# Two-block parts, resident activations and doubled statistics in a mixed feed-forward after local attention

## The reference

```
x = x + LN(attention(LN(x), w_qkv))                    # 4 x 2048 tokens of width 512, window 128
x = x + LN(ffn(LN(x)))                                 # LN: layer norm over the width, no gain
ffn(y):                                                # for each of 4 batches b
  g   = mean_s(relu(y @ gate_w1.T + gate_b1) @ gate_w2.T + gate_b2)      # 8 numbers for a batch
  mW1 = W1 + sum_e g[e] TW1[e]; mb1 = b1 + g @ Tb1      # 8 experts, mixed into one matrix
  mW2 = W2 + sum_e g[e] TW2[e]; mb2 = b2 + g @ Tb2
  out = gelu(y @ mW1.T + mb1) @ mW2.T + mb2             # hidden width 2048
```

## Time and profile before

| what | value |
|---|---|
| time of the profiled execution | 3095.89 us |
| its span | 3094.1 us |
| mean granted TensorE clock | 0.974 |
| TensorE busy | 2929.2 us (95%) |
| VectorE busy | 1999.8 us (65%) |
| ScalarE busy | 1520.0 us (49%) |
| GpSimd busy | 880.2 us (28%) |
| data moved | 814.49 MB |

### The profile page before, as it was taken

How to read it: one execution, slowest core, us unless ns; L and a number is a source line. 1 busy time by engine, 2 the same in 40 slices (tenths; PEclk the granted TensorE clock), 3 DMA queues, 4 the chain that set the end, 5 groups by cost and what they waited for, 6 DMA issues and landing times.

```text
span 3094.1 us, 55462 instructions
## 1 busy us (share of the span) xinstructions
PE 2929.2 (95%) x20444; PEld 2425.8 (78%) x20444; DVE 1999.8 (65%) x3732; ACT 1520.0 (49%) x2950; POOL 880.2 (28%) x773
## 2 busy tenths in 40 slices
PE   7999999789999999959888899999999999999997
PEld 5888888578888888847776688878888888888886
DVE  4333333278888888857756677798868766897412
ACT  2222222167666666745534455554445544554444
POOL 0000000178888888853310000140005100240004
PEclk9999999889999999979988999999999999999999
DMA  5554554567877777669999999999989988999533
GB/s 190 177 176 163 180 194 167 162 167 197 197 194 186 195 193 188 172 205 363 354 354 348 334 378 381 355 404 403 394 302 352 366 301 316 361 372 356 202 109 123
DMA packets 444433, 814.49 MB, mean 263 GB/s; under 512 B 29705, under 2 KB 161801, under 8 KB 444185
## 3 DMA queue, kind: packets, MB, share of 16 engines
q1 hardware_dynamic: 360800, 630.95, 61.8%
q10 hardware_dynamic: 73920, 146.81, 13.3%
q0 software_dynamic: 9472, 33.56, 2.9%
HBM read 642.89 MB, written 167.78 MB: 262 GB/s over the span
## 4 chain that ended last, share of the span: by engine, by line
PE 42%; DMA 7%; DVE 3%; ACT 1%; issue 1%; POOL 1%; SPq 1%; POOLq 0%; ACTq 0%; DVEq 0%
PE e_hid L1190 7%; PE e_hid L1191 7%; PE e_hid L1192 7%; PE e_acc L1209 7%; PE e_acc L1207 7%; PE e_acc L1208 7%; DMA yl_scratch<-e_yt_lo 4%; DMA e_y_lo<-yl_scratch 3%; DVE e_yt_lo L1441 1%; DVE e_part L1491 1%; DVE e_c_stats L1414 1%; SPq L976 0%; DVE e_c_y L1435 0%; ACT e_yt_hi L1269 0%; POOL e_sums L1111 0%
## 5 line engine op out<-in xcount | busy, mean ns | idle before, releaser
L1491 DVE SCALAR_TENSOR_TENSOR e_part<-e_ring,e_g_cols,e_part 128x512 f32<-128x512 f32 x896 | 659.2, 794 | 6.6 <-DMA e_ring<-mix_rows 4.0
L666 DVE TENSOR_REDUCE b_neg_max<-b_ps_score 128x1 f32<-128x384 f32 (+1 forms) x1024 | 491.7, 527 | 67.6 <-PE b_ps_score L531 56.1
L1305 ACT ACTIVATE e_u<-e_hid,e_mb 128x512 f32<-128x512 f32 x256 | 176.5, 689 | 647.7 <-PE e_hid L1192 644.8
L637 ACT ACTIVATE b_probs<-b_ps_keys 128x384 f32<-128x384 f32 (+1 forms) x1024 | 426.8, 478 | 78.8 <-PE b_ps_keys L546 51.1
L1515 DVE TENSOR_TENSOR e_u_lo<-e_u,e_u_hi 128x512 fp32r<-128x512 f32 x256 | 186.7, 729 | 374.0 <-ACT e_u_hi L1309 373.9
L1099 POOL TENSOR_SCALAR e_var<-e_moments 128x4 f32<-128x4 f32 x16 | 8.1, 504 | 1199.5 <-DVE e_moments L1526 1199.5
L531 PE MATMUL b_ps_score<-b_k_st,b_q_st 96*128 96x384 f32 (+1 forms) x1024 | 333.3, 366 | 15.4 <-DMA b_q_st<-qk_scratch 15.1
L491 POOL TENSOR_TENSOR b_total<-b_probs 128x512 f32<-128x512 f32 x256 | 323.8, 1280 | 64.8 <-ACT b_probs L637 64.8
L546 PE MATMUL b_ps_keys<-b_q_st,b_k_st 97*128 97x384 f32 (+1 forms) x1024 | 315.1, 350 | 23.8 <-DMA b_q_st<-b_max_rows 22.4
L1190 PE MATMUL e_hid<-e_y_hi,e_wb_hi 128*128 128x512 f32 x784 | 308.7, 394 | 22.4 <-DMA e_y_lo<-yl_scratch 13.5
L237 DVE TENSOR_TENSOR a_qk<-a_acc,a_qk 128x512 fp32r<-128x512 f32 x128 | 88.6, 692 | 357.6 <-ACT a_qk L176 356.6
(11 more groups left out here) (137 smaller groups left out, 5837.1 us busy)
## 6 DMA issues: line engine op xcount, KB each, us to landing
e_ring<-mix_rows SPq DMA_DIRECT2D x558, 512.0 KB, 8.9
e_y_hi<-yh_scratch ACTq DMA_DIRECT2D x70, 1024.0 KB, 11.2
e_y_lo<-yl_scratch ACTq DMA_DIRECT2D x70, 1024.0 KB, 17.2
qk_scratch<-a_qk SPq DMA_DIRECT2D x128, 512.0 KB, 2.7
b_k_st<-qk_scratch SPq DMA_DIRECT2D x192, 256.0 KB, 4.2
b_q_st<-qk_scratch SPq DMA_DIRECT2D x192, 256.0 KB, 4.2
a_x_in<-x SPq DMA_DIRECT2D x16, 1024.0 KB, 7.0
v_scratch<-a_v SPq DMA_DIRECT2D x64, 256.0 KB, 3.0
```

The costliest lines, as they stand in the source:

```text
L637: act.activation(probs[:, m % RING, h, 0:(hi - lo) * WIN], ps_keys[x % BANKS][:, 0:(hi - lo) * WIN], ACT.Exp, scale=SCALE).then_inc(exp_do ...
L666: dve.tensor_reduce(neg_max[:, g % 2, i, h:h + 1], ps_score[y % BANKS][:, 0:(hi - lo) * WIN], AX_X, ALU.max, negate=True).then_inc(reduced, 1)
L1491: dve.scalar_tensor_tensor(out=part[:, n % 2, half, :], in0=ring[:, slot, :], scalar=g_cols[:, b, e:e + 1], in1=so_far, op0=ALU.mult, op1= ...
```

## The change

Every unit has two blocks, so that there are 128 runs of two steps in place of 72 of two to four. All four chunks of y of a batch have a place on chip and are loaded once for a batch: chunks 0 and 1 of batch 0 by SP as before, now behind the last transposes of the gate, chunks 2 and 3 by SP behind refill_half(1) and refill_half(2), and those of the next batch by ScalarE after the last hidden_block of the closing run that has the same chunk. W_RING falls from 9 to 5. The statistics have two buffers, used in turn by closing runs, and row_stats waits for the closing run before the last. The wait for the stores of y of all chunks moves from SP to ScalarE's first copy_out.

```diff
-W_RING = 9
+W_RING = 5
...
-    return [(0, 0, 2), (0, 2, 2), (0, 4, 3), (0, 7, 3), (0, 10, 3), (0, 13, 3)] + \
-        [(b, 4 * quarter, 4) for b in range(1, BATCH) for quarter in range(4)]
+    return [(b, j, 2) for b in range(BATCH) for j in range(0, FF // P, 2)]
...
-        stats = sb("stats", [P, TILES, 6], F32)
+        stats = sb("stats", [P, 2, TILES, 6], F32)
...
-        y_hi = sb("y_hi", [P, 2, KD, CH], F32R)
-        y_lo = sb("y_lo", [P, 2, KD, CH], F32R)
+        y_hi = sb("y_hi", [P, PER, KD, CH], F32R)
+        y_lo = sb("y_lo", [P, PER, KD, CH], F32R)
...
-        def load_y(eng, r):
+        def load_y(eng, b, q):
+
+            rows = slice((PER * b + q) * CH, (PER * b + q + 1) * CH)
             for src, dst in ((yh_dram, y_hi), (yl_dram, y_lo)):
-                eng.dma_start(dst[:, r % 2].bitcast(F32),
-                              src[:, tokens(r)].rearrange("(k p) t -> p k t", p=P)).then_inc(y_loaded[r % 2], 16)
+                eng.dma_start(dst[:, q].bitcast(F32),
+                              src[:, rows].rearrange("(k p) t -> p k t", p=P)).then_inc(y_loaded[q], 16)
...
                         sp.wait_ge(x1_done, TILES * CHUNKS)
-                        sp.wait_ge(yt_stored[0], 32)
-                        load_y(sp, 0)
-                        sp.wait_ge(yt_stored[1], 32)
-                        load_y(sp, 1)
+                        sp.wait_ge(turned, KD * CHUNKS)
+                        for q in range(2):
+                            sp.wait_ge(yt_stored[q], 32)
+                            load_y(sp, 0, q)
...
-                for p in range(2):
-                    sp.wait_ge(yt_stored[p], 32 * CHUNKS // 2)
+                sp.wait_ge(yt_stored[0], 64)
+                load_y(sp, 0, 2)
                 refill_half(2)
+                sp.wait_ge(yt_stored[1], 64)
+                load_y(sp, 0, 3)
...
-                    if jj == 0:
-                        pe.wait_ge(y_loaded[r % 2], 32 * (r // 2 + 1))
+                    q = runs[r][1]
+                    if jj == 0 and opens(r):
+                        pe.wait_ge(y_loaded[q], 32 * (batch_of(r) + 1))
...
-                    if s == last[r] and r + 2 < RUNS:
-                        load_y(act, r + 2)
+                    if s == last[r] and closes(r) and b + 1 < BATCH:
+                        load_y(act, b + 1, runs[r][1])
...
                         act.wait_ge(bias_done, biases_by(1))
+                        for p in range(2):
+                            act.wait_ge(yt_stored[p], 32 * CHUNKS // 2)
...
-                    if at:
-                        dve.wait_ge(norm_done, TILES * at)
+                    i = at % 2
+                    if at >= 2:
+                        dve.wait_ge(norm_done, TILES * (at - 1))
```

More of the change, by code:

```diff
@@ L833, in phase_gate_ffn @@
         unused = sb("unused", [P, TILES], F32)
-        stats = sb("stats", [P, TILES, 6], F32)
-        moments = sb("moments", [P, TILES, 2], F32)
-        var = sb("var", [P, TILES], F32)
-        rstd = sb("rstd", [P, TILES], F32)
-        shift = sb("shift", [P, 2, TILES], F32)
+        stats = sb("stats", [P, 2, TILES, 6], F32)
+        moments = sb("moments", [P, 2, TILES, 2], F32)
+        var = sb("var", [P, 2, TILES], F32)
+        rstd = sb("rstd", [P, 2, TILES], F32)
+        shift = sb("shift", [P, 2, 2, TILES], F32)
         c_b1 = sb("c_b1", [P, KD], F32)
@@ L925, in phase_gate_ffn @@
         table_ready = sem("table_ready")
-        y_loaded = [sem(f"y_loaded{i}") for i in range(2)]
+        y_loaded = [sem(f"y_loaded{i}") for i in range(PER)]
         mix_done = sem("mix_done")
@@ L1344, in normalise @@
                         rows = sums[:, runs[r][1], t, :]
-                        act.activation(rows, rows, ACT.Identity, bias=shift[:, 1, t:t + 1], scale=rstd[:, t:t + 1]).then_inc(norm_done, 1)
+                        act.activation(rows, rows, ACT.Identity, bias=shift[:, at % 2, 1, t:t + 1], scale=rstd[:, at % 2, t:t + 1]).then_inc(norm_done, 1)
                 for k in range(-3, CHUNKS):
```

19 lines of the change are left out of this document (10 added, 9 removed).

## The result

The changed kernel takes 3103.23 us (median of 20 runs, 3095.61 to 3113.23), the kernel before 3095.36 in the runs beside it: ratio 1.0024, 95% interval 1.0013 to 1.0034. It is slower by 0.24%, 7.9 us; forecast were 18.7 us. Its profiled execution was its longest, 3113.23 us with a span of 3111.3. How much it loses is known no better than to some 0.2%.

The account below looks back on a forecast made before the run. TensorE was taken to bound the feed-forward, so only its waits and the slow clock behind them could be won. Removed -33.1, closing runs +35.1, tail +16.7 make +18.7 us: 3114 us, range 3084 to 3136.

Parts of the forecast that it names:

- The removed waits: Batch 0: TensorE's waits for y (20.2 us with slow clock) and for block 6 (8.9 us) go.
- moved at no cost: SP's later y loads and stores, and W_RING = 5, would stay covered and cost nothing.
- The closing runs: Ends of batches 0 to 2: late GpSimd costs 11.7 us a batch, 35 in all; the old pattern's 4.0 us go.
- The clock: Behind the stalls at ends of batches 0 to 2: two groups at lower clock, 3.6 us a batch.
- The cycle: GpSimd's time for a closing run beside mixes: 14.6 us against runs 10.9 us apart, fourth run 11.0 us late.
- What is absorbed: Closing steps: slack at normalise (0.6 us) and last preload (2.3 us) takes up 2.9 us, leaving 8.1 us of stall.
- the forecast's own range: Whole kernel, if the forecast itself holds: 3102 to 3124 us, chance 0.45.
- The tail: After the last matmul: nothing hides GpSimd's closing runs, cycle 11.1 us, so the tail grows by 16.7 us.
- GpSimd keeping up: Rival, closing steps of batches 0 to 2: cycle below about 11.9 us, no stall left, 3079 us; chance 0.12.
- half of it: Rival, closing steps: thin mixes, cycle about 13 us, 5.1 us lost a batch, 3094 us; chance 0.23.
- Late transfers of y: Rival, batch starts: next batch's y loads compete with other transfers and come late, +34 us, 3129 us; chance 0.2.
- the rule that the prediction took from the Trainium skill: GpSimd-issued transfers starve while VectorE holds the shared port pair; stores would land later, adding 15 us.

Follow-up runs that it names:

- e16: Changed kernel with weight slots 0 and 1 moved between two halves of the small tensors: 3110.92 us, one run.
- e10: Changed kernel with ring and part moved to the top of the partition and weight slots 0 and 1 at the bottom: 3101.70 us, ratio 1.0037.
- e11: Changed kernel with the mixing plan's price of a closing run raised from 3.4 to 8.5 us: 3091.68 us, ratio 0.9987.
- e4: Changed kernel with GpSimd's addition of x1 cut from 512 to 8 columns of each tile: 3080.42 us, ratio 0.9956.
- e1: Changed kernel with the last two parts of the last batch made one part of four blocks: 3089.23 us, ratio 0.9981.
- e9: Changed kernel with weight slots 0 and 1 moved to the top of the partition, behind u_lo: 3089.38 us, ratio 0.9985.
- e12: Changed kernel with weight slots 0 and 1 moved 11.7 KB up, behind the small tensors: 3089.47 us, ratio 0.9994.
- e15: Changed kernel with x1, bias and the small tensors moved behind u_lo: 3091.47 us, one run.
- e18: The kernel of e12 with w2g (128 bytes) behind weight slots 0 and 1 in place of before them: 3100.86 us, ratio 1.0026.
- e3: Kernel before with parts of two blocks everywhere and nothing else, y still loaded for each run: 3392.38 us, ratio 1.0989.

## Why the forecast was too high

**The removed waits: right.** -28.6 us for -29.1 in the first 128 groups, and +2.0 of the slower slots is in it, so the waits and what hung on them gave some 30.6. W_RING = 5 brought no wait for a block, y none for a load. But the "moved at no cost" was incomplete: five slots put more groups on the two slow ones.

**The closing runs: right in mechanism, wrong in size. This is the step that failed.** Predicted were 11.7 us a batch, 8.1 of stall and 3.6 of two groups at the lower clock, 35.1 in all, less the old pattern's 4.0: +31.1. Measured were +4.0, +6.9 and +7.1, together +18.0, of which 1.6 come from the slower slots. Counted above the pace of unhindered groups, the new pattern costs 21.5 us: 14.9 of waits for the 24.3 of stall, 5.1 in the six groups behind them for the 10.8 at the lower clock, 1.5 around them. Three sizes were off:
- The clock. Of the six groups at the lower clock one came, 4.52 us behind the 4.1 us wait of batch 0 in place of 2.80, 1.7 us. The other five took 3.42 us at 1.00, 0.6 to 0.7 us too much each, for the preloading one by one. That the clock had fallen behind a wait of 2.1 us was carried over to waits of 1.9 to 2.3 us, where it did not fall. It might have: other traces show waits of this length with either outcome, so one slow group was no ground for a term of two in each batch. (Two groups at the 1.9 us of the rows are 3.8, not 3.6.) The first group below stands behind a wait of 1.86 us in e16, the second behind one of 2.63 us in e10:

```profile
2380.90:2385.56 4.66, 4.66 (x12) 3.38 (x13) 4.66 (x6) 3.63 (x7) 4.48 (x7) 0.63 0.99 368
2383.10:2386.50 3.40, 3.36 (x12) 2.17 (x13) 3.40 (x2) 3.37 (x7) 3.38 (x5) 1.00 1.03 416
```

- The cycle. It was taken from one closing run as 14.6 us; in batch 1 it was 14.0, so the fourth run came 42.0 us after the first in place of 43.8, and 1.6 of the 42.0 are ScalarE's, behind VectorE's mix. In batch 0 it was 15.8, 15.0 and 13.8, and part of that was not the additions but x1 landing late (4.45, 3.45 and 1.23 us of wait; 3.80 in batch 1), which the working did not have.
- What is absorbed. With 14.0 the fourth run is 3 x (14.0 - 10.94) = 9.2 us late in batch 1, and TensorE stood for 4.3 of it: 4.9 us were absorbed, not 2.9. e11 agrees: 39.0 - 32.8 = 6.2 us late, 1.4 stood, 4.8 absorbed.

e4 shows the cause (0.3 us of wait with small additions), e11 what the mixes in the closing steps have to do with it (5.4 us with next to none there). That the number still fell into the forecast's own range (from 3102) is in part luck: a loss that was not foreseen at all, the slots, made up for a part of what was priced too high.

**The tail: right.** +15.4 us for +16.7; the cycle without mixes was 11.0 for 11.1, and the first of the four runs came a little earlier than counted. e1 gives it back whole.

**Left out: the place of the weights.** +8.5 us, 4.9 of them in stretches without a wait. By the earlier trace rows all groups were taken as alike, at 2.71 to 2.74 us; the two kinds of them, 2.72 and 2.80, stood in the trace of before.

**The sum.** By the rows of the table, from 18.7: -13.1 for the ends of batches, +6.9 for the stretches between and behind them, +0.5 for the first 128 groups and -1.3 for the tail make 11.7; TensorE's part and tail of the two traces give -3.5 + 15.4 = 11.9. The medians differ by 7.9. The other 4 us stay open: they are within the 16 us by which the start of the feed-forward moved, and the y waits of the kernel before may be longer in other executions than in the one that was profiled.

**The rivals.** GpSimd keeping up was priced at 3079, and did not come. That e4, with small additions, takes 3080 is a coincidence: its tail is 10.4 us shorter, which the rival's sum had not, and it has the slower slots. The median of 3103 lies between "half of it" (3094) and the forecast (3114), and in mechanism too: a cycle of 14 us, and one group at the lower clock. Late transfers of y kept nothing waiting, though e4 shows one that would have (3.6 us) if TensorE had come earlier; only x1 landed late. Of the rule that the prediction took from the Trainium skill (SBUF — State Buffer, "SBUF: two separate sides") the trace shows nothing in the stores: they landed within 14.6 us, and no opening run waited for one. The page says this of VectorE operations in a mode that takes both ports; whether the mixes are of this kind no run here shows. The x1 loads, which GpSimd issues too, did keep it waiting, for 16.2 us; but with next to no mixes beside them (e11) it waited 17.6 us, so the mixes are not shown to delay them.

## What to carry to other kernels

When work of a fixed cycle (here 11 to 14 us on GpSimd) is brought to one end of a loop, compare its cycle with the spacing of the runs, and keep the last parts of the last batch large: one line was worth 14 us. A hand-made plan that prices VectorE's work alone is wrong where GpSimd adds beside it; raising the price of a closing run from 3.4 to 8.5 us, which is nearer to what was measured, was worth 11 us. Before anything else is tuned on a kernel bound by TensorE, sort its matmuls by operand and look at the distance of their starts: here some 6 ns a matmul, 29 us in all by the traces, hung on the order and the sizes of declarations.

## What the runs showed of the hardware

- Matmuls of 512 columns, 4 bytes each, followed each other after 227 ns where the places of stationary and moving operand agreed within 512 bytes (e9, e12, e15, wb everywhere), and after 231 to 234 where the weights' place less that of y, u or xt was 32 (changed kernel), 192 (before), 320 (e16), 384 (e18) or 480 bytes (first phase; 32 the other way round), at the same granted clock of 1.00 and without a wait. It cost the changed kernel 16 to 17 us in the feed-forward and some 13 in the first phase. The mechanism behind it was not looked into.
- What the clock does behind a wait of some 2 us of TensorE isn't settled by the wait's length. In the changed kernel it stayed at 1.00 behind waits of 1.9 to 2.3 us and was 0.62 over the group behind one of 4.1 us; but it was 0.63 behind 1.86 us (e16), 0.62 behind 1.90 and 1.00 behind 2.39 us (both e18), 1.00 behind 2.63 us (e10) and behind 3.20 us (e3).
- Six mixes took 9.20 us on VectorE beside GpSimd's additions and 4.06 without; with next to none of them in the closing steps, GpSimd's cycle was 11.6 us in place of 14.1 where x1 had landed in time.
